# A macaron transformer block: a small load awaited at its first use, GpSimd's and VectorE's work put in another order, the last products and the last store in two

## The reference

```python
def ffn(x, w_gate, w_up, w_down):          # weights int32, times 1/127; hidden width 768
    h = silu(x @ wg.T) * (x @ wu.T)
    return h @ wd.T
def attn(q, Wq, Wk, Wv, Wo, bo):
    scores = qh @ kh.T * D**-0.5 - slopes * abs(i - j)
    return softmax(scores) @ vh @ Wo.T + bo
x = x + 0.5 * ffn(layernorm(x))
x = x + attn(layernorm(x))
x = x + 0.5 * ffn(layernorm(x))
```

## Time and profile before

| | us |
|---|---|
| median of 3 runs | 853.54 |
| the runs | 854.68, 847.97, 853.54 |
| the profiled execution | 846.51 |
| its span, first to last instruction | 844.6 |
| TensorE, mean granted clock in the span | 0.991 |

### The profile page before, as it was taken

One profiled execution on the slowest core, in us unless ns is written; L12 is line 12 of the kernel. 1 busy time (PEld: TensorE's weight loads), 2 busy tenths in 40 slices (PEclk: granted clock), 3 DMA queues, 4 the chain that ended last, 5 costly groups with the idle time before them and its releaser, 6 DMA issues.

```text
span 844.6 us, 13093 instructions
## 1 busy us (share of the span) xinstructions
PE 785.2 (93%) x4576; PEld 492.3 (58%) x4576; DVE 621.9 (74%) x1259; ACT 509.1 (60%) x745; POOL 477.9 (57%) x574
## 2 busy tenths in 40 slices
PE   2599999898999999999999999999999899999997
PEld 2478888675444454454454454454454367878886
DVE  6389887978779768768768678678878447677764
ACT  4234454335757867867877777778767764444433
POOL 0244344435755866866965965966666554444433
PEclk9799999999999999999999999999999999999999
DMA  9330005503431450550640730720620000000001
GB/s 360 131 42 3 2 12 78 66 2 43 75 57 23 73 72 10 84 69 2 96 56 3 105 49 3 112 40 18 97 40 1 3 2 27 26 28 28 27 28 51
DMA packets 21491, 43.18 MB, mean 51 GB/s; under 512 B 3848, under 2 KB 5912, under 8 KB 21208
## 3 DMA queue, kind: packets, MB, share of 16 engines
q1 hardware_dynamic: 21400, 41.92, 27.2%
HBM read 12.02 MB, written 4.62 MB: 20 GB/s over the span
## 4 chain that ended last, share of the span: by engine, by line
PE 80%; DVE 9%; issue 4%; DMA 3%; ACT 2%; SPq 1%; POOL 0%; DVEq 0%; ACTq 0%
PE ps L981 74%; DVE hid L795 3%; PE ps L1044 2%; DMA q_scale<-q_scale 2%; DVE row_max L861 2%; PE ps L993 1%; DVE newton L727 1%; PE ps L1049 1%; PE ps L1039 1%; DVE rstd L729 1%; DVE newton L725 1%; ACT probs L680 1%; PE ps L1019 1%; SPq L365 1%; ACT stage L627 1%
## 5 line engine op out<-in xcount | busy, mean ns | idle before, releaser
L861 DVE TENSOR_REDUCE row_max<-ps 128x1 f32<-128x512 f32 x512 | 329.9, 685 | 106.1 <-PE ps L981 104.6
L680 ACT ACTIVATE probs<-ps 128x1024 f32<-128x1024 f32 x256 | 262.6, 1029 | 74.9 <-PE ps L981 74.2
L548 POOL TENSOR_TENSOR probs<-probs,diag 128x256 f32<-128x256 f32 x256 | 187.5, 734 | 150.7 <-ACT probs L680 150.5
L456 POOL TENSOR_TENSOR hid_r<-hid,hid_r 128x512 fp32r<-128x512 f32 x96 | 124.5, 1299 | 190.9 <-ACT hid_r L575 190.2
L981 PE MATMUL ps<-k_aug,q_aug 60*128 60x512 f32 x512 | 208.5, 468 | 13.3 <-issue 6.4
L981 PE MATMUL ps<-xnt,wgu_r 128*128 128x512 f32 x768 | 193.5, 405 | 19.4 <-DVE hid L795 15.0
L981 PE MATMUL ps<-q_aug,k_aug 62*128 62x512 f32 x512 | 191.2, 452 | 2.7 <-ACT probs L680 2.7
L981 PEld LDWEIGHTS ps<-xnt,wgu_r 128*128 128x128 f32 x768 | 144.0, 192 | 60.2 <-DVE hid L795 20.4
L981 PEld LDWEIGHTS ps<-q_aug,k_aug 62*128 62x128 f32 x512 | 80.2, 185 | 140.4 <-issue 122.3
L581 ACT ACTIVATE gated<-ps 128x512 f32<-128x512 f32 x96 | 57.3, 598 | 131.3 <-PE ps L981 122.0
L981 PE MATMUL ps<-probs,v_aug 128*32 128x512 f32 x1024 | 136.3, 605 | 0.0
(11 more groups left out here) (73 smaller groups left out, 683.4 us busy)
## 6 DMA issues: line engine op xcount, KB each, us to landing
q_aug<-parts SPq DMA_DIRECT2D x96, 128.0 KB, 4.6
k_aug<-parts SPq DMA_DIRECT2D x96, 128.0 KB, 4.6
x_sb<-x_in SPq DMA_DIRECT2D x8, 512.0 KB, 13.0
x_out<-x_sb SPq DMA_DIRECT2D x8, 512.0 KB, 2.6
diag<-diag_table SPq DMA_DIRECT2D x1, 2048.0 KB, 18.8
wgu_i<-w_gate_up SPq DMA_DIRECT2D x2, 768.0 KB, 6.1
w_att<-w_att SPq DMA_DIRECT2D x1, 1024.0 KB, 11.4
q_aug<-max_parts SPq DMA_DIRECT2D x64, 8.0 KB
```

Source lines behind the costliest of these rows:

```text
L456: nc.gpsimd.tensor_tensor(hid_r[:, 1, f, :], hid[:, f % 2, :], hid_r[:, 0, f, :].bitcast(F32), ALU.subtract).then_inc(s["hid_lo"], 1)
L548: nc.gpsimd.tensor_tensor(tile, tile, diag[:, kt % 2, n * QH + 2 * pair:n * QH + 2 * pair + 2, :], ALU.mult).then_inc(fixed, 1)
L680: nc.scalar.activation(probs[:, kt % 2, 2 * pair:2 * pair + 2, :], ps[:, at:at + 2, :], ACT.Exp, scale=SLOPE_UNITS[pair]).then_inc(exp_don ...
L861: nc.vector.reduce_max(row_max[:, quad % 2, i, pair, t:t + 1], max_bank(tile), mybir.AxisListType.X).then_inc(s1_used, 1)
```

## The change

Six edits. ScalarE waits for q_scale inside `empty` for the first qk0. SP lays the q rows of both sides at once and the k rows of side 1 where both stood (side 1's k rows lie in memory that stage one uses). GpSimd's `split_max` comes after the multiplication of step (n,3), ahead of that step's other piece. The normalising of sequence b+2 goes to (0,4), (0,5), (0,6) and (1,5). Stage two's gather and links 0 to 3 come at the end of the turn before (turn 0: at its start), links 4 to 7 ahead of hid f=0, 8 to 11 behind it; turn 7 has none. In `down`, the first maxima of stage one's last turn are transposed at f = 1, not 0, and the last turn of stage two finishes tiles 0 and 1 before 2 and 3; the last sequence is stored in two halves.

```diff
-APPLY_AT = {(1, 2): 0, (1, 4): 1, (1, 6): 2, (2, 2): 3}
+APPLY_AT = {(0, 4): 0, (0, 5): 1, (0, 6): 2, (1, 5): 3}
@@ SP
-            lay_rows(0)
+            lay_q_rows(0)
+            lay_k_rows(0)
+            lay_q_rows(1)
...
             sp.wait_ge(ffn[0]["y_used"], 2 * B)
-            lay_rows(1)
+            lay_k_rows(1)
...
-            def store(b):
-                sp.wait_ge(ffn[1]["y_used"], 2 * b + 2)
-                sp.dma_start(d_out[b], x_of(b, 0, TT)).then_inc(stored, 16)
-            for b in range(B):
-                store(b)
-            sp.wait_ge(stored, 16 * B)
+            def store(b, tile, n):
+                sp.wait_ge(ffn[1]["y_used"], 2 * b + (tile + n) // 2)
+                sp.dma_start(d_out[b][:, tile * C:(tile + n) * C], x_of(b, tile, n)).then_inc(stored, 16)
+            for b in range(B - 1):
+                store(b, 0, TT)
+            store(B - 1, 0, 2)
+            store(B - 1, 2, 2)
+            sp.wait_ge(stored, 16 * (B + 1))
@@ GpSimd
-                        if name and name.startswith("max"):
-                            split_max(b, name)
                         pool.wait_ge(exp_done, g + 1)
...
                                                 ALU.mult).then_inc(fixed, 1)
+                        if s == 3 and FILLS[n, 4] in fills_of(b):
+                            split_max(b, FILLS[n, 4])
@@ ScalarE
                     if kind == "qk" and part % 2 == 0:
+                        if name == "qk0_next" and b < 0:
+                            act.wait_ge(scale_in, 16)
...
-            act.wait_ge(scale_in, 16)
             turns(act, lambda b: ffn_turn(0, b))
@@ VectorE
+            def gather_ahead(b):
+
+                ready = att_done + one * b + TT
+                stats_ready(ready)
+                ln_gather((0,))
+                ln_links(ready + TT, (0,), range(4))
...
-                slots = (0,) if w == 1 or first(b) else (0, 1) if not last(b) else ()
+                slots = () if w == 1 else (0,) if first(b) else (0, 1) if not last(b) else ()
...
+                if w == 1 and then:
+                    if first(b):
+                        gather_ahead(b)
+                    ln_links(at, (0,), range(4, 8))
                 for f in range(FT):
...
+                    if w == 1 and then and f == 0:
+                        ln_links(at, (0,), range(8, LINKS))
...
                 if not last(b):
                     turned(w, b + 1)
+                if w == 1 and b < B - 2:
+                    gather_ahead(b + 1)
@@ TensorE
             def down(weights, dtype, w, b):
...
+                if w == 1 and last(b):
+                    for j, fs in ((0, range(0, 5)), (1, range(0, 3)), (0, range(5, 6)), (1, range(3, 6))):
+                        for f in fs:
+                            down_part(weights, dtype, w, b, f, (2 * j, 2 * j + 1))
+                    return
...
-                        if f == 0:
+                        if f == 1:
                             fill(-1, "max0_next")
```

More of the change, by code:

```diff
@@ L376, in _, with lay_q_rows @@
             sp.wait_ge(rows_in, 16 * 2)
-            def lay_rows(side):
+            def lay_q_rows(side):
                 for i in range(2):
@@ L381, in lay_rows, with lay_k_rows @@
                                  ).then_inc(aug_in[side], 16)
+            def lay_k_rows(side):
+                for i in range(2):
                     sp.dma_start(k_aug[side][i * GROUP + ROW_BIAS:i * GROUP + ROWS, :, :].bitcast(F32),
@@ L772, in _ @@
             att_done = a_done + (2 * TT + LINKS) + one
+            def gather_ahead(b):
[3 more added lines that the diff above has]
+                ln_links(ready + TT, (0,), range(4))
             def ffn_turn(w, b):
                 s = ffn[w]
-                slots = (0,) if w == 1 or first(b) else (0, 1) if not last(b) else ()
+                slots = () if w == 1 else (0,) if first(b) else (0, 1) if not last(b) else ()
                 if w == 1:
-                    ready = att_done + one * b + (0 if last(b) else TT)
+                    ready = att_done + one * b + TT
                 elif first(b):
@@ L783, in ffn_turn @@
                 then = not last(b)
-                at = ready + TT * len(slots)
+                at = ready + TT * (1 if w == 1 else len(slots))
+                if w == 1 and then:
+                    if first(b):
+                        gather_ahead(b)
+                    ln_links(at, (0,), range(4, 8))
                 for f in range(FT):
@@ L1132, in gate_up, with down_part @@
                         scores_for_max(0, FIRST_MAX_AT[b, f])
+            def down_part(weights, dtype, w, b, f, tiles):
+                s = ffn[w]
+                for part in range(2):
+                    pe.wait_ge(s["hid_lo" if part else "hid_hi"], FT * b + f + 1)
+                    for t in tiles:
+                        out = ps[:, y_at + t // 2, (t % 2) * C:(t % 2 + 1) * C]
+                        tokens = hid_r[:, part, f, t * P:(t + 1) * P]
+                        ins = matmul(out, tokens if dtype == F32R else tokens.bitcast(F32), weights[:, f, :],
+                                     f == 0 and part == 0 and t % 2 == 0, f == FT - 1 and part == 1,
+                                     skip_group_check=True)
+                        if f == FT - 1 and part == 1 and t % 2 == 1:
+                            ins.then_inc(s["y_done"], 1)
             def down(weights, dtype, w, b):
                 s = ffn[w]
+                if w == 1 and last(b):
[3 more added lines that the diff above has]
+                    return
                 for f in range(FT):
@@ L1147, in down @@
                             scores_for_max(0, FIRST_MAX_DOWN[f])
[L1148 to L1158, removed]
+                    down_part(weights, dtype, w, b, f, range(TT))
             pe.wait_ge(eye_in, 16)
```

## The result

The changed kernel takes 825.68 us (median of four runs, 824.33 to 828.79) against 851.53 for the kernel before (four runs, 847.97 to 854.68): a ratio of 0.970, interval 0.965 to 0.976, which is 25.3 us less (25.9 between the medians). The prediction was 822.0, range 814 to 835. The profiled execution took 824.33, its span is 822.4 against 844.6: 22.2 us less, where the sum of the prediction had 27.7. So the direction, the range and the order of the terms held; the terms themselves did not all hold, and two of the errors are more instructive than the total.

A forecast was written before the change was run, and what follows sets the result against it. TensorE, busy 93% of the span, was taken to bound the kernel. Terms 11.0 + 1.0 + 6.2 + 2.6 + 6.0 + 0.9 = 27.7 us took the profiled 846.5 to 818.8; the median was forecast at 822, range 814 to 835.

The forecast's parts named there:

- q_scale: Start of stage one: without ScalarE's wait TensorE need not stop and its clock stays up; 11.0 us, bounds 8.7 and 11.8.
- rival (c): Start: the clock stays low, so only 8.7 of 11 us are gained, 825 us; chance 0.06.
- what is late next?: Start, q_scale's term: x for later batches, wanted by VectorE at about 38 us, was issued ahead of q_scale, landed at 30.2.
- max0: Passage to attention: eight matmuls of down f=0 fill TensorE's 1.7 us idle; 1.0 us gained, bounds 0.5 and 1.7.
- rival (d): Attention, quad 0: normalising collides with VectorE by the shared port, TensorE waits in six batches; slower, 855 us; chance 0.02.
- The wait for `rows_moved`: Attention step (2,3): rows leave 1.07 us sooner; 6.2 us over six stalls, 2.6 in batch 0 with its low clock.
- Rival (a): Attention step (2,3): the stall stays because DMA engines bound the rows; loses 6 to 8 us, 829; chance 0.12.
- Normalising, side 1's rows: Attention: normalisings move where GpSimd idles, with 2.5 us cover, and row transfers move where SP idles; no cost or gain.
- Stage two: Stage two's turns: moved links remove the f=5 stall, 0.6 us a steady turn; 6.0 us, bounds 3 and 6.4.
- the end: Last down and store: 0.4 us from one x_sb operation fewer, 0.5 from half a transfer; 0.9 us, bounds 0.3 and 1.5.
- rival (b): Stage two: VectorE becomes late at the turn, the gain there is 1 to 2 us instead of 6.0; 826; chance 0.10.
- the 7 us that the median lies above the profiled execution stay: Whole kernel: if the median's 7.0 us excess stays, 826; if it sat in a wait now gone, 819; middle 822.

The follow-up runs named there:

- 1.000 alone: The kernel before with only the normalising moved into quad 0: 851.44 us, ratio 1.000 (0.998 to 1.003).
- the experiment: The kernel before with only stage two's gather and links moved: 843.2 us, ratio 0.993 (0.991 to 0.996).
- the copy: The kernel after with GpSimd copying its own value instead of taking the maximum over the partitions: 826.1 us, ratio 0.971 (0.965 to 0.977).
- a probe: The kernel after with small GpSimd operations ahead of and behind the maximum over partitions: 835.58 us; with later loads held back too, 832.94 us; one run each.

## Why the prediction was right, point by point

**q_scale, 11.0 predicted, 9.1 measured in the two profiled executions, 8.1 on the mean of nine traces.** The first SiLU came at 19.60, 1.3 us sooner than worked out, TensorE did not stop ahead of f=2, and its matmuls came 0.23 us apart from 21.3 on; rival (c) fell. By the last matmul of f=3 TensorE was 11.2 us ahead; it lost 2.0 of them in two stops. The step that failed is "what is late next?": I asked it of SP's transfers alone, and it was GpSimd. In the kernel before its first subtraction at 32.27 followed hid at once, since the wait for q_scale had left it 17 us behind the maximum over the partitions. The trace of before could not show when GpSimd would have been ready, and I put no bound on it. Idle times of 0.97 and 0.82 us are that error.

**max0, 1.0 predicted, a loss measured.** The idle time went as costed (1.70 to 0.56; attention's first scores 9.66 us sooner, 0.6 more than at `turn_x`). But I stopped at the transpose. The step that failed is that nothing behind it would change: GpSimd's additions now fell beside the normalisings, and the next late thing, a row maximum, came 0.5 us later: 1.06 + 0.31 us of idle time in two pieces before, 1.47 in one after, with low clock behind it. The row maximum cost 0.4 us, the low clock behind it 4.0, and much of that is chance between these two executions, as the traces above show. I had the port's rule in the text for stage two and for rival (d), and did not hold it against the bias additions.

**The wait for `rows_moved`: 2.6 and 6.2 predicted, 3.6 and 8.8 measured** (1.43 to 1.49 each), of which batch 6 gave 1.3 back, when a wait for a row maximum that had lain beside the old one (0.87 us) came to the front. Mechanism right, size wrong: I priced a stall at TensorE's idle time of 0.99 to 1.13. The weight load of the same matmul had stood longer, 1.39 us at 421.20 in batch 3 and up to 1.53 in the others, as the row of PEld would have told. Rival (a) fell: the transfers were not held up by those of qk0. But they take most of the time: in both traces the six of k_aug land about 1.0 us apart, the last 8.5 us after the first issue before (421.14) and 8.2 after (409.06), and TensorE comes for it at 409.28. The stall is gone with 0.2 us to spare.

**Normalising, side 1's rows: nothing predicted, nothing measured.** GpSimd's normalisings at 385 to 391 delay multiplications that have cover; (d) fell, 1.000 alone.

**Stage two, 6.0, and the end, 0.9: together 7.1 measured.** Split by the experiment: 5.5 and 1.6. Stage two by its own steps: 17.7 us a turn as forecast, no link of 1.2 us in any steady turn (only turn 0, whose links stand at its start, still has one), cover at hid f=0 even larger; rival (b) fell. The end was sized by half a transfer (0.5) and half a hand-over (0.4): the kernel ends 3.1 us after the last x_sb starts at 819.26, where it ended 4.4 us after the two x_sb had started at 840.24.

**The median.** I took 822 as the middle between "the 7 us that the median lies above the profiled execution stay" and "they go". The scatter now has two named sources, the stop in stage two (about 5 us, in six of fourteen traces) and low clock behind idle times (1.7 to 6.8 us, at different places in each). Both belong to executions, though the low clock follows idle times, some of which the change removes. The 50 runs of the kernel before that stand beside these experiments bear the second out: the longer the run, the lower its mean granted clock (correlation -0.90; 845.2 us on the mean at 0.993, 854.7 at 0.983). The gain of the medians is 25.9 us, nearer to the sum than the 22.2 of the two profiled executions, since the profiled one of before lay 5.0 us below its median and that of after only 1.4. That the median fell at 825.7 and not lower is no proof of the terms: q_scale was put 2 to 3 us too high and the passage 4.8, `rows_moved` 3.6 too low, of which the waits that came to the front took 2.6 back.

## What to carry to other kernels

When a first wait goes, ask of every engine, not of the transfers alone, when it would have been ready without it; an engine that had seventeen idle microseconds ahead of an instruction may have needed ten of them. Price a stall by the weight load's idle time, and look at the next late thing on its other side. Before crediting 3 us to an edit, see whether executions of one kernel differ by that at a place the edit doesn't touch. And when an experiment shows a start time, ask first what it waited for: the subtraction behind the copy was late against the copy, but not against its input.

## What the runs showed of the hardware

At the start GpSimd stood 5.8 us ahead of the maximum over the partitions and 7.3 us behind it with the DMA engines idle; with them at some 410 GB/s it stood 9.7 us ahead of it, and in the kernel after it was not ready for 10.4 us behind it. The first copy, cast and operation with a scalar had no such pause. TensorE started with matmuls 0.43 us apart and went over to 0.23 at 20.6 to 23.7 us, another time in each of the twelve traces without a probe. TensorE can stand 2.38 to 2.95 us in the middle of a down, in one execution and not in the next; that a block of its instructions comes late there is inferred from the packet's time. And an idle time of 0.72 us for a row maximum in batch 0 was followed by 3.4 us of half clock in the kernel after (0.57 over 250 to 254). So it was in seven of the ten traces in which the wait for `rows_moved` ahead of it is gone, and in none of the four that still have that wait, where the half clock lies behind the wait.
